# Perceiver block: cross-attention scores on row tiles of TensorE, and an opening by channel chunks

## What is computed

```
q = layernorm(x) @ Wq.T + bq        # 256 tokens, 16 heads of 32 channels
k = ctx @ Wk.T + bk                 # 4096 tokens
v = ctx @ Wv.T + bv
scores = clip(q . k / sqrt(32), -50, 50)   # masked tokens get -50
probs  = softmax(scores);  ctx_out = probs @ v
x = x + layernorm(rs * (ctx_out @ Wo.T + bo)) * gamma + beta
```

## Time and profile before

| | us |
|---|---|
| median of 3 runs | 826.15 (825.44 to 826.71) |
| profiled execution, its own time | 824.42 |
| its span in the trace | 822.7 |
| TensorE busy in the span | 747.9 (91%) |
| VectorE busy | 602.8 (73%) |
| ScalarE busy | 405.5 (49%) |

### The profile page before, as it was taken

One profiled execution on the slowest core, in us unless ns is written; L12 is line 12 of the kernel. 1 busy time (PEld: TensorE's weight loads), 2 busy tenths in 40 slices (PEclk: granted clock), 3 DMA queues, 4 the chain that ended last, 5 costly groups with the idle time before them and its releaser, 6 DMA issues.

```text
span 822.7 us, 15196 instructions
## 1 busy us (share of the span) xinstructions
PE 747.9 (91%) x5776; PEld 476.5 (58%) x5776; DVE 602.8 (73%) x955; ACT 405.5 (49%) x536; POOL 12.8 (2%) x35
## 2 busy tenths in 40 slices
PE   4995999999999999847599995789999999999997
PEld 2642555554555455415377772567777777777774
DVE  5474888888888786443588885468888888888885
ACT  4363566657666656501366663234444444444442
POOL 1200000000000000000000000000000000000000
PEclk9998999999999999987799999689999999999999
DMA  7469050605051323022014400077676677777770
GB/s 284 119 210 298 3 120 36 154 0 153 1 153 30 76 54 101 27 114 91 1 78 153 153 26 0 4 246 230 232 247 228 227 237 244 231 229 234 246 230 28
DMA packets 37031, 113.72 MB, mean 138 GB/s; under 512 B 8528, under 2 KB 18176, under 8 KB 34432
## 3 DMA queue, kind: packets, MB, share of 16 engines
q1 hardware_dynamic: 36448, 112.64, 43.5%
q0 software_dynamic: 256, 0.52, 0.3%
q10 hardware_dynamic: 288, 0.02, 0.0%
HBM read 94.73 MB, written 0.57 MB: 116 GB/s over the span
## 4 chain that ended last, share of the span: by engine, by line
PE 71%; issue 16%; DVE 4%; DMA 3%; SPq 3%; ACT 1%; POOL 0%; DVEq 0%; POOLq 0%; ACTq 0%
PE pS L974 32%; PE pP L974 23%; PE pD L974 8%; PE pO L974 8%; DMA arena<-in_ctxT 2%; SPq L279 1%; DMA arena<-in_wkT 1%; PE pS L986 1%; SPq L229 1%; ACT arena L493 0%; DVE bn L648 0%; DMA arena<-w_scratch 0%; DVE arena L681 0%; ACT xT L425 0%; SPq L251 0%
## 5 line engine op out<-in xcount | busy, mean ns | idle before, releaser
L974 PE MATMUL pS<-arena 128*128 128x256 f16 (+2 forms) x2706 | 335.8, 279 | 7.9 <-DVE arena L768 3.7
L974 PEld LDWEIGHTS pS<-arena 128*128 128x128 f16 (+1 forms) x2706 | 270.8, 102 | 81.5 <-issue 13.4
L974 PE MATMUL pP<-arena 128*128 128x512 f16 x984 | 240.1, 385 | 19.6 <-DVE arena L662 10.6
L974 PEld LDWEIGHTS pP<-arena 128*128 128x128 f16 x984 | 92.8, 99 | 146.4 <-issue 36.8
L493 ACT ACTIVATE arena<-pS,mblk 128x1024 f32<-128x1024 f32 x128 | 146.9, 1201 | 4.7 <-PE pS L974 4.4
L887 DVE SCALAR_TENSOR_TENSOR arena<-arena 128x1536 f16<-128x1536 f32 x72 | 126.1, 1752 | 2.4 <-ACT arena L590 2.4
L723 DVE TENSOR_SCALAR arena<-arena 128x1024 f32<-128x1024 f32 x128 | 88.2, 693 | 47.6 <-ACT arena L493 47.2
L607 ACT ACTIVATE arena<-pS 128x256 f32<-128x256 f32 x72 | 27.6, 383 | 164.3 <-PE pS L974 164.3
L590 ACT ACTIVATE arena<-arena 128x1536 f16<-128x1536 f32 x72 | 106.3, 1477 | 0.0
L974 PE MATMUL pO<-arena 128*32 128x256 f32 (+4 forms) x1216 | 85.8, 365 | 3.7 <-DVE arena L847 3.1
L974 PE MATMUL pD<-arena 128*128 128x512 f16 x312 | 81.2, 379 | 4.8 <-DVE arena L949 3.3
(11 more groups left out here) (166 smaller groups left out, 461.0 us busy)
## 6 DMA issues: line engine op xcount, KB each, us to landing
arena<-in_units SPq DMA_DIRECT2D x72, 768.0 KB, 4.8
arena<-arena SPq DMA_DIRECT2D x112, 128.0 KB, 2.4
arena<-w_scratch SPq DMA_DIRECT2D x144, 64.0 KB, 2.6
arena<-in_ctxT SPq DMA_DIRECT2D x8, 1024.0 KB, 6.1
mw_in<-in_mla_in SPq DMA_DIRECT2D x8, 1024.0 KB, 6.7
mw_out<-in_mla_out SPq DMA_DIRECT2D x8, 512.0 KB, 3.3
arena<-arena SPq DMA_DIRECT2D x32, 64.0 KB, 2.0
arena<-in_wkT SPq DMA_DIRECT2D x1, 1024.0 KB, 5.0
```

What stands on the lines that cost most here:

```text
L974: return pe.matmul(o, lhsT, rhs, start=start, stop=stop, **kw)
```

## The change

1. **Scores on row tiles.** `k_st` and `q_st` and all stacking DMAs go. PE reads kh, kl, qh and ql where DVE wrote them: the 4 heads j of a group lie in the partitions 32j to 32j+31, and each matmul has 32 rows. A step is 12 matmuls of 256 columns: the three parts kh by qh, kl by qh, kh by ql in turn, and in each part the four heads one after another, each in its own row group and its own bank. A step's results take half of each of the four banks of pS.
2. **Steps in pairs.** `scores` now does steps 2i and 2i+1 together, waits for the exponentials of both steps of the pair before, and signals once behind both.
3. **kh and kl have two buffers** (b % 2); the waits for stacks in `split_k` are gone.
4. **Opening by chunks.** wk and context block 0 come in 4 DMAs of 256 KB each, in turn by channel chunk. ACT splits wk and the context chunk by chunk, DVE too, ahead of the mask table. PE runs 10 matmuls on zeros as soon as POOL has cleared `zero16` (now its first memset), then works chunk by chunk on all four k units in four banks, with the transposes within the last chunk; then q; then the v units, two at a time. ACT evacuates all four k units before it splits wv.
5. SP issues the mask, the small rows, wqa, wkva and the MLA weights right behind `prep_ready`.

```
         def unit_bank(b, n):
-            return (pP if n % 2 == 0 or not (isinstance(b, int) and b == 0) else pD)[:, :]
+            if isinstance(b, int) and b == 0:
+                return (pP[:, :], pD[:, :], pO[:, 0, :], pO[:, 1, :])[n % 4]
+            return pP[:, :]
         def step_scores(st):
-            return pS[:, 2 * (st % 2):2 * (st % 2) + 2, :].rearrange("p b (h q) -> p (b h) q", h=2)
+            return pS[:, :, T * (st % 2):T * (st % 2) + T]
...
-            sp.dma_start(wk32, a["wkT"]).then_inc(s["wk_in"], 16)
-            load_ctx(0, 0)
+            for c in range(HC):
+                sp.dma_start(wk32[:, c], a["wkT"][:, c]).then_inc(first_in[c], 16)
+                sp.dma_start(cbuf[:, 0, c], a["ctxT"][0][:, c]).then_inc(first_in[c], 16)
...
             sp.wait_ge(s["prep_ready"], 1)
             load_mask(0, 0)
-            stack_k0(0, s["k0_stacked"])
-            sp.wait_ge(s["q_lo"], 1)
-            stack_q(sp, 2, 4, s["q_rest"])
-            stack_k0(2, s["k0_rest"])
...
+            pool.memset(zero16[:, :], 0.0).then_inc(s["zero_ready"], 1)
...
+            for c in range(HC):
+                act.wait_ge(first_in[c], 32)
+                act.activation(wk16[:, 0, c], wk32[:, c], ACT.Copy, scale=SW).then_inc(s["wk_hi"], 1)
+                split_ctx(0, c)
+            transposed(1)
+            act.wait_ge(s["prep_ready"], 1)
+            for n in range(HC):
+                evac(0, 0, n)
...
-                        act.wait_ge(s["scores_done"], STEPS * b + st + 1)
+                        act.wait_ge(s["scores_done"], PAIRS_X * b + i + 1)
...
             for n in range(HC):
                 dve.wait_ge(s["wk_hi"], n + 1)
+                dve.scalar_tensor_tensor(wk16[:, 1, n], wk32[:, n], SW, wk16[:, 0, n], ALU.mult, ALU.subtract)\
+                   .then_inc(s["wk_lo"], 1)
+                split_ctx(0, 0, n)
...
+            pe.wait_ge(s["zero_ready"], 1)
+            for _ in range(10):
+                mm(pS[:, 0, :], zero16[:, 0:128], zero16[:, :], True, True)
+            for c in range(HC):
+                pe.wait_ge(s["wk_lo"], c + 1)
+                pe.wait_ge(s["ctx_lo"], c + 1)
+                for n in range(HC):
+                    if c == HC - 1 and n == 2:
+                        pe.wait_ge(s["const_ready"], 1)
+                        transpose_rows(1)
+                    unit_part(unit_bank(0, n), 0, n, c)
...
+            for n in (HC, HC + 2):
+                pe.wait_ge(s["proj_evac"], n - HC + 2)
+                for c in range(HC):
+                    pe.wait_ge(s["wk_lo"], HC + c + 1)
+                    unit_part(unit_bank(0, n), 0, n, c)
+                    unit_part(unit_bank(0, n + 1), 0, n + 1, c)
...
-            def scores(b, p, st):
-                g, tile = st // CT, st % CT
-                if not (isinstance(b, int) and b == 0 and st < 2):
-                    pe.wait_ge(s["exp_done"], STEPS * b + st - 1)
-                for j in range(4):
-                    last = mm(step_scores(st)[:, j, :], k_st[:, p, j, g, 128 * tile:128 * tile + 128],
-                              q_st[:, j, g, :], True, True)
+            def scores(b, p, i):
+                first = isinstance(b, int) and b == 0
+                if first and i % 2 == 0:
+                    pe.wait_ge(s["k_lo"], i // 2 + 1)
+                if not first and i == 0:
+                    pe.wait_ge(s["k_lo"], 4 * (b + 1))
+                if not (first and i == 0):
+                    pe.wait_ge(s["exp_done"], STEPS * b + 2 * i)
+                for st in (2 * i, 2 * i + 1):
+                    g, tile = st // CT, st % CT
+                    for k, (w, x) in enumerate(((kh, qh), (kl, qh), (kh, ql))):
+                        for j in range(4):
+                            r = slice(32 * j, 32 * j + 32)
+                            last = mm(step_scores(st)[:, j, :], w[r, p, g, 128 * tile:128 * tile + 128], x[r, g, :],
+                                      k == 0, k == 2)
                 last.then_inc(s["scores_done"], 1)
```

More of the change, by code:

```diff
@@ L116, in build @@
         wv16 = take(2 * HC * HID, f16).rearrange("p (s c n) -> p s c n", s=2, c=HC)
-        kh = take(HC * CB, f16).rearrange("p (g t) -> p g t", g=HC)
-        kl = take(HC * CB, f16).rearrange("p (g t) -> p g t", g=HC)
+        kh, kl = (take(2 * HC * CB, f16).rearrange("p (b g t) -> p b g t", b=2, g=HC) for _ in range(2))
         kf = take(2 * CB).rearrange("p (b t) -> p b t", b=2)
@@ L126, in build @@
         psums = (psum4, xT[:, :, :])
[L127 to L131, removed]
+        wk32, wv32 = (take(HC * HID).rearrange("p (c n) -> p c n", c=HC) for _ in range(2))
         qh, ql = (work[:, i, :].bitcast(f16).rearrange("p (g q) -> p g q", g=HC) for i in range(2))
@@ L215, in build @@
         s = {n: sem(n) for n in names}
+        first_in = [sem(f"first_in{i}") for i in range(HC)]
         ctx_in = [sem(f"ctx_in{i}") for i in range(2)]
@@ L221, in build @@
         wb_in = [sem(f"wb_in{i}") for i in range(RING)]
[L223 to L229, removed]
         block = ctx.enter_context(nc.Block())
@@ L469, in _ @@
             act.wait_ge(ctx_in[1], 16)
-            for n in range(3, 7):
+            for c in range(HC):
+                split_ctx(1, c)
+            for n in range(HC, 2 * HC):
                 evac(0, 0, n)
-                split_ctx(1, n - 3)
-            evac(0, 0, 7)
             def x_block(b, p, proj=True, split=True, dve_sums=True):
@@ L988, in transpose_rows, with unit_part @@
                 last.then_inc(s["tr_done"], 1)
+            def unit_part(bank, p, n, c):
+                for k, (wi, ci) in enumerate(((0, chi), (1, chi), (0, clo))):
+                    start, stop = c == 0 and k == 0, c == HC - 1 and k == 2
+                    if n < HC:
+                        last = mm(bank, wk16[:, wi, c, 128 * n:128 * n + 128], ci[:, p, c, :], start, stop)
+                    else:
+                        r = n - HC
+                        last = mm(bank, ci[:, p, c, 128 * r:128 * r + 128], wv16[:, wi, c, :], start, stop)
+                if c == HC - 1:
+                    last.then_inc(s["proj_done"], 1)
@@ L990, in project @@
             def project(b, p, n):
-                first = isinstance(b, int) and b == 0
-                if n == 0 and not first:
+                if n == 0:
                     pe.wait_ge(s["ctx_lo"], 4 * (b + 1))
-                if first:
-                    if n < HC:
-                        pe.wait_ge(s["wk_lo"], n + 1)
-                    if n >= 2:
-                        pe.wait_ge(s["proj_evac"], n - 1)
-                else:
-                    pe.wait_ge(s["proj_evac"], 8 * b + n)
@@ L1002, in project @@
-                bank = unit_bank(b, n)
-                k = 0
-                for c in range(HC):
-                    if first and n == 0:
-                        pe.wait_ge(s["ctx_lo"], c + 1)
-                    if first and n == HC:
-                        pe.wait_ge(s["wk_lo"], HC + c + 1)
-                    for wi, ci in ((0, chi), (1, chi), (0, clo)):
-                        if n < HC:
-                            last = mm(bank, wk16[:, wi, c, 128 * n:128 * n + 128], ci[:, p, c, :], k == 0, k == 11)
-                        else:
-                            r = n - HC
-                            last = mm(bank, ci[:, p, c, 128 * r:128 * r + 128], wv16[:, wi, c, :], k == 0, k == 11)
-                        k += 1
@@ L1070, in x_block @@
                 first = isinstance(b, int) and b == 0
-                if first:
-                    pe.wait_ge(s["k0_stacked"], 16 * STACK_DMAS)
-                else:
-                    pe.wait_ge(s["k_stacked"], 16 * STACK_DMAS * b)
                 for i in range(PAIRS_X):
-                    if first and i == HC:
-                        pe.wait_ge(s["k0_rest"], 16 * STACK_DMAS)
-                    scores(b, p, 2 * i)
-                    scores(b, p, 2 * i + 1)
+                    scores(b, p, i)
                     if i:
```

85 lines of the change are left out of this document (18 added, 67 removed).

## The result

| | before, us | changed, us |
|---|---|---|
| median of 4 runs each, same chip | 826.27 (825.44 to 826.71) | 815.0 (814.01 to 816.73) |
| profiled execution, its own time | 824.42 | 816.73 |
| its span | 822.7 | 815.2 |

The ratio is 0.9867 [0.9847, 0.9887]: faster by 11.3 us in the medians, where 20 were forecast. 815.0 lies inside the range of 801 to 818, but outside the 802 to 811 of the prediction's own case. In the profiled executions the difference is 7.7 us, since the profiled one of the changed kernel is its slowest of four.

The account below looks back on a forecast made before the run. TensorE was taken to bound the kernel, busy 91% of the span, plus a 9.1 us gap. Terms -6.6 + 2.5 - 10.6 - 5.25 = -19.95 us gave 804.5 profiled, 806.2 us median; range 801 to 818.

Parts of the forecast that it names:

- the prediction's own case: Whole kernel: all terms as summed, 806.2 us, reaching from 802 to 811; given 59%.
- longer rounds: Rival on the scores: four weight loads may not hide, rounds of 0.142 us, +12 us, 818 us; 15%.
- an opening that gains nothing: Rival on the opening: slow chunks or xn late, 811 to 813 us; 10%.
- Row tiles: Scores: four row groups at once, rounds of 0.109 us, net -0.12 us a turn, -6.6 us over 56 turns.
- Both rivals on rounds: Scores: row groups only two by two, 847 us, 8%; or rounds of 0.142 us, 818 us, 15%.
- Gap and last block: Block 0's gap goes through earlier context block 2, -10.6 us; last block's exponential-score ring of 3.25 us, +2.5 us.
- VectorE has 3.94 us of work a turn, against 4.67: still covered, and late next.: Cross-attention turns with a project: VectorE's work still fits the shorter turn, so no cost was counted.
- TensorE's shorter turn meets DVE or ACT: Rival on turns with a project: clips come late, turns stay at 4.79 us, 813 us; 8%.
- The opening: Start of kernel: chunked loads, first real matmul near 6.5 us, first scores at 35.1 instead of 40.35, -5.25 us.
- the tightest point: Opening: mask table and norm end at 15 us, TensorE wants xn at 15.6; waiting for chunks would show error.
- the stacks' POOL and SP issues have no other cost: Removed stacking DMAs: beyond the gap in block 0, their issues on POOL and SP cost nothing else.
- The ten on zeros take that, if zeros count as work: Opening: zero matmuls from 1.5 to 6 us absorb the slow-clock start; if not, 1.3 us comes back.

Follow-up runs that it names:

- Experiment 6: Kernel before with only the load of context block 2 moved ahead of all stacks; 817.56 us, ratio 0.9883.
- experiments 1: Changed kernel with TensorE's loop over blocks 1 to 4 written out, no jump back; 810.86 us, ratio to before 0.981.
- split before sums (4): Changed kernel with VectorE splitting the last context chunk ahead of turn 7's sums; 810.98 us, ratio to before 0.9825.
- heads outer (5): Changed kernel with score loops exchanged, so each head's three parts run in a row on one row group; 816.65 us in one run.
- changed again (10): The changed kernel itself once more, unaltered, beside the last experiment on one chip; 814.19 us, ratio to before 0.9852.
- 11: Changed kernel with TensorE's loop written out, context split before the sums, and POOL's selrow held until xn is ready; 809.83 us, ratio to before 0.9812.
- experiment 9: Changed kernel with twenty zero matmuls of 256 columns in place of ten of 512; 815.98 us, ratio to before 0.9872.
- old opening (7): Changed kernel with the opening of before: 1 MB loads, units in turn, no zeros; 815.92 us, ratio to before 0.9876.
- no zeros (8): Changed kernel without its ten matmuls on zeros; 813.83 us, ratio to before 0.9856.
- before, matmuls cut (3): Kernel before with looped-block matmuls cut by columns, giving 1861 TensorE instructions a pass, same products; 829.43 us, ratio 1.0038.

## Why the prediction was right, and where it was wrong

**The range: right in part by luck.** 815.0 is 8.8 us above the forecast of 806.2 and outside the prediction's own case, which ended at 811. The range went on to 818 for longer rounds, an opening that gains nothing and turns that stay at 4.79 us. None of the three came as described (of the last, a third did); other costs, which no term had, filled their place.

**Row tiles: right.** "So two row groups run at once" extended to four: rounds of 0.109 us, 24 matmuls in 0.83. Both rivals on rounds fall. By the 3.07 times that the Trainium skill gives for four row tiles ("TensorE: Matmul & The Clock Gate", part 3) a round would be 0.142, the estimate of the prediction; that figure is for 512 columns. Here it is 0.109 with 256 columns, four at once at full rate, and no run has row tiles of 512. The wait for the pair costs nothing where there is a project, and one more change of tiling costs the 0.10 us assumed.

**Gap and last block: right**, to 0.1 us. Experiment 6 shows by itself that the gap comes from the late issue of this one load.

**"VectorE has 3.94 us of work a turn, against 4.67: still covered, and late next."** This step failed in its first half. 3.94 is a mean over turns; in turn 7 VectorE has its clips, two sums and the last split of the context, in this order, and the split has a due time of its own, the first project of the next block. Of the rival "TensorE's shorter turn meets DVE or ACT" this is the part that came: 2.1 us of the 6.6 it had, in 5 turns. The time from the end of L662 to the start of that project in the kernel before, turn by turn, would have found it: 0.19 us at the start of block 1.

**The opening: mechanism right, size off by 1.7 us.** The term was "the first real matmul at about 6.5" and scores at 35.1; it measured 7.19 and 36.79. ACT in time, on the chunks:

```profile
5.09 0.63 ACT L415 ACTIVATE arena<-arena 128x512 f16<-128x512 f32 x1 [2.08 <-DMA arena<-in_ctxT]
...
6.91 0.63 ACT L415 ACTIVATE arena<-arena 128x512 f16<-128x512 f32 x1 [0.67 <-DMA arena<-in_ctxT]
...
9.91 0.63 ACT L415 ACTIVATE arena<-arena 128x512 f16<-128x512 f32 x1 [0.25 <-DMA arena<-in_ctxT]
```

The first pair of chunks is there at 5.09, not 4.5, and the next (the third is at 8.51) come 1.8, 1.6 and 1.4 us apart, where the rate of 1 MB DMAs gave 1.3: a small price for 256 KB DMAs, far from the 2.1 us each at which the prediction had 7.6 us lost. TensorE needs a pair every 2.6 us and never waits for a chunk again. Then it waits 0.61 us for xn, "the tightest point", as named (and by its last paragraph a sign of being wrong): the norm took 1.39 us in place of 1.00, with POOL's `selrow` beside it from 15.41 to 16.14. With `selrow` moved it takes 1.00. The change itself had brought the two together: in the kernel before, `selrow` stands behind POOL's stacking DMAs and runs at 35.85. So "the stacks' POOL and SP issues have no other cost" missed this. From 7.19 to 36.79 are 29.6 us where 28.6 were forecast: these 0.61, and 0.4 spread over the rest.

**The zeros: undecided, not right.** "The ten on zeros take that, if zeros count as work" holds in the first profile of the changed kernel and in those of experiments 1, 4 and 5, but not in those of experiments 10 and 11, where the same ten end at 5.84 too and the first real matmuls have the spacing of the lower level (1.23 us for three, where 0.65 is that of 2.4 GHz). Where they take, first scores come 0.4 to 1.1 us earlier than without them (36.62 to 37.29 against 37.70); where not, at about the same time (37.61, and 37.34 with `selrow` moved). The busy times by stretch are no help: they say 1.00 from 5.8 to 9.5 us in both cases, since they take 1.00 where the trace has no clock record. The trace's clock records start, at the upper level, at 5.5 to 6.6 us in the four and at 10.8 and 10.1 us in the two. With twenty zero matmuls of 256 columns (experiment 9) the granted clock is 0.80 from 5.8 to 9.5 us, only the first three matmuls are fast, and first scores come at 37.73. The length of the idle time behind the ten doesn't decide it: 1.22 to 1.35 us in the four, 1.05 and 1.25 in the two. What decides was not found.

**What no step had: the number of TensorE's instructions.** This is the largest part of the miss, 6.6 us of the 12.4 in the profiled executions (4.4 in the second profile of the changed kernel). The prediction counts matmuls by their time alone. The change turns 640 matmuls of a pass into 896, with as many weight loads; nothing in the sum asked whether that number mattered. The rows for it were in the trace of before: q8's transfers in the first pass, and none in the second. The Trainium skill has the mechanism, "Runtime: NRT & Kernel Launch", section "Instruction fetch mechanics": TensorE's memory holds 2048 instructions, refilled in blocks of 256, and a branch taken to a target outside the current window of two blocks has to fetch it before execution goes on. The trace agrees with the block (16384 bytes, one for about 256 instructions) and with the cost of the branch (4.74 us against 0.25). It doesn't agree with the sizes: by a window of two blocks a pass of 1349 would not be held, and it was; by 2048 instructions one of 1857 would be, and it was not.

**What stays open.** Why the stall is 6.6 us in one kernel and 1.9 in the next, with the same number of instructions in the loop, and 6.6 and 4.4 in two profiles of the same kernel. The traces say this much (q8 is counted over the 2.2 us behind the start of the branch; "clock falls" is a granted clock under 1.00 behind the jump):

| kernel | branch, us | q8 blocks | idle, us | clock falls | lost, us |
|---|---|---|---|---|---|
| changed | 4.74 | 2 | 1.55 + 1.98 | yes | 6.6 |
| changed again (10) | 3.59 | 1 | 0.39 + 1.93 | yes | 4.4 |
| split before sums (4) | 4.81 | 2 | 1.61 + 1.71 | yes | 5.4 |
| short zeros (9) | 4.48 | 2 | 1.29 + 2.16 | yes | 5.35 |
| heads outer (5) | 4.38 | 2 | 1.19 + 1.68 | no | 3.35 |
| old opening (7) | 3.31 | 1 | 1.06 | no | 1.9 |
| no zeros (8) | 3.45 | 1 | 0.26 + 1.28 | no | 2.2 |
| before, matmuls cut (3) | 3.79 | 1 | 1.93 + 0.37 | no | 2.65 |

The branch takes 4.4 to 4.8 us where two blocks are fetched behind it at once and 3.3 to 3.8 where it is one; where the clock falls, the next twelve matmuls take 3.62 to 4.49 us in place of 2.76. What makes it two blocks is open, and so is why the clock falls in experiment 10 and not in 5, which idles longer. Where the jump falls within a block of 256 is one guess, and experiment 9 speaks against its simplest form, as do the two profiles of one kernel.

The stretch behind the cross-attention, +1.6 us in the table, was 477 to 481 us long over all kernels, whatever was changed: that term is within their scatter, and no cause was found. A finer wait in the last block (step by step, to open its ring) was not tried: in the changed layout the results of two steps in turn share their banks.

## What to carry to other kernels

When a change makes more and smaller instructions in a loop, count the instructions of a pass on each engine, not only their time, and look whether the DMA queue that fetches that engine's instructions (q8 here) falls silent in the second pass; if it does, ask whether it still will after the change, and if it won't, write the loop out. Check an engine that is "covered on average" at the one turn where its work bunches, against the due time of that turn's last product. And when the largest term of a gain is one late load, try that load alone first: here it gave some 9 of the 11 us, and uncovered a 2 us wait.

## What the runs showed of the hardware

- A loop of 1349 TensorE instructions passes a second time without fetches, and its jump back takes 0.25 us; one of 1857 or 1861 fetches 16384 bytes every 8 to 13 us away from the jump, its jump back takes 3.3 to 4.8 us, and TensorE loses 1.9 to 6.6 us there; the same work written out doesn't stall.
- Row groups of TensorE don't keep program order among each other: 24 matmuls on four groups take 0.83 us in the order of groups and 0.85 with three in a row on each (the latter in one run).
- Ten matmuls on zeros, 1.39 to 5.84 us, all at the spacing of the lower level, were followed by matmuls at the upper level in four profiles of six (experiment 5's zeros end at 5.72).
- A POOL affine select of 128 x 512 beside two VectorE operations with a per-partition operand: 1.39 us for the two instead of 1.00.
